# Eight-chunk groups, a ring of 32 slots and one-comparison one-hots in a graph-convolution and expert kernel

## The reference, cut to what matters

```python
def gcn_conv(x, W, b, src, dst, n_nodes):
    loop = jnp.arange(n_nodes)
    s = jnp.concatenate([src, loop])
    d = jnp.concatenate([dst, loop])
    deg = jax.ops.segment_sum(jnp.ones(s.shape[0]), d, num_segments=n_nodes)
    dinv = jnp.where(deg > 0, jax.lax.rsqrt(deg), 0.0)
    xw = x @ W
    msg = xw[s] * (dinv[s] * dinv[d])[:, None]
    return jax.ops.segment_sum(msg, d, num_segments=n_nodes) + b
```

## Time and profile before

| | |
|---|---|
| median of 3 runs | 6199.94 us (6199.23 to 6201.64) |
| profiled execution, its span | 6262.0 us, 79540 instructions |
| layer 1 gathers, 217.5 to 2681.3 us | 2463.8 us |
| between the layers, 2681.3 to 2761.7 us | 80.4 us |
| layer 2 gathers, 2761.7 to 5227.5 us | 2465.8 us |
| before, and behind them | 217.5 us, 1034.5 us |

### The profile page before, as it was taken

The page is one execution under the profiler, slowest core; times in us unless marked ns, Lnnn a source line. Parts: engine busy times, 40 slices in busy tenths (PEclk is TensorE's granted clock), DMA queues, the critical chain, the costliest instruction groups (busy, mean ns, idle before and its releaser), DMA issues.

```text
span 6262.0 us, 79540 instructions
## 1 busy us (share of the span) xinstructions
PE 4364.0 (70%) x15129; PEld 2132.3 (34%) x15130; DVE 1873.3 (30%) x7104; ACT 1178.2 (19%) x2841; POOL 3402.7 (54%) x3639
## 2 busy tenths in 40 slices
PE   4667766676676666666666766667667666669999
PEld 4322222222222222232222222222222223458888
DVE  7311121111121111241122221212121215657776
ACT  5200000000000000030000000001000003545555
POOL 0466666666666666636666666666666663331111
PEclk5676676666666777676776666766666667779999
DMA  3633333333333333343333333333333233331111
GB/s 112 208 106 90 88 88 88 88 89 88 88 90 89 89 87 88 89 126 90 87 90 88 88 89 89 87 89 89 89 87 90 86 90 86 88 116 49 51 48 46
DMA packets 261631, 564.59 MB, mean 90 GB/s; under 512 B 67215, under 2 KB 136177, under 8 KB 261554
## 3 DMA queue, kind: packets, MB, share of 16 engines
q0 software_dynamic: 171168, 466.40, 25.7%
q1 hardware_dynamic: 89234, 95.13, 5.4%
q10 hardware_dynamic: 1152, 2.20, 0.1%
HBM read 503.38 MB, written 60.10 MB: 90 GB/s over the span
## 4 chain that ended last, share of the span: by engine, by line
PE 25%; issue 15%; another core or an unknown queue 14%; DMA 5%; DVEq 4%; POOL 3%; DVE 3%; ACT 2%; ACTq 0%; POOLq 0%; SPq 0%
PE ps L1708 10%; PE ps L1914 7%; DMA ring<-messages,idx_stage 5%; PE ps L1929 3%; POOL ring L645 3%; PE ps L1606 2%; DVEq L1169 2%; DVE onehot_mem L1161 2%; PE ps L1729 1%; PE ps L1833 1%; DVEq L1161 1%; ACT acc L825 0%; ACT dinvT L857 0%; DVEq L1170 0%
## 5 line engine op out<-in xcount | busy, mean ns | idle before, releaser
L645 POOL DMA_INDIRECT ring<-messages,idx_stage x3328 | 3159.0, 949 | 1935.8 <-issue 883.7
L1708 PE MATMUL ps<-ring,onehot_mem 128*64 128x256 f32 x6656 | 2801.3, 544 | 1255.3 <-DMA ring<-messages,idx_stage 621.4
L1708 PEld LDWEIGHTS ps<-ring,onehot_mem 128*64 128x64 f32 x6656 | 950.1, 180 | 2751.8 <-DMA ring<-messages,idx_stage 1650.1
L1172 DVE TENSOR_TENSOR acc<-acc,ps 128x128 f32 x832 | 240.3, 289 | 3795.7 <-remote 2064.5
L779 ACT ACTIVATE win_rows<-ps 64x256 f32<-64x256 f32 x832 | 313.7, 378 | 2224.7 <-PE ps L1708 1106.2
L1161 DVE TENSOR_SCALAR onehot_mem<-iota_bf,tables 128x64 f32<-128x64 bf16 x3344 | 641.8, 268 | 187.5 <-issue 125.7
L1606 PE MATMUL ps<-ident,win_rows 64*128 64x64 f32 x1664 | 337.9, 296 | 368.3 <-ACT win_rows L779 295.7
L768 ACT ACTIVATE idx_stage<-tables 128x8 int32 (+1 forms) x420 | 87.4, 209 | 2276.7 <-PE ps L1708 981.1
L1606 PEld LDWEIGHTS ps<-ident,win_rows 64*128 64x128 f32 x1664 | 206.3, 173 | 867.8 <-issue 867.8
L1914 PE MATMUL ps<-acc 128*128 128x256 f32 x2016 | 459.0, 380 | 0.8 <-ACT acc L955 0.8
L704 POOL DMA_INDIRECT out_dram<-acc x126 | 125.7, 998 | 579.1 <-DVE acc L1556 399.1
(11 more groups left out here) (264 smaller groups left out, 2072.9 us busy)
## 6 DMA issues: line engine op xcount, KB each, us to landing
ring<-messages,idx_stage POOLq DMA_INDIRECT x3328
rows_mem<-in_x_dram SPq DMA_DIRECT2D x54, 448.0 KB, 3.8
acc<-routed_rows SPq DMA_DIRECT2D x63, 268.0 KB
messages<-dinvT SPq DMA_DIRECT2D x23, 448.0 KB, 6.2
dinvT<-in_x_dram SPq DMA_DIRECT2D x22, 448.0 KB, 4.4
messages<-ring SPq DMA_DIRECT2D x19, 448.0 KB, 4.0
dinvT<-dinv_row SPq DMA_DIRECT2D x28, 224.0 KB
messages<-rows_mem SPq DMA_DIRECT2D x14, 448.0 KB, 4.0
```

The source lines that it names most:

```text
L645: pool.indirect_dma_start(out=slots[:, s, :], out_offset=None, in_=t_dram[layer], in_offset=bass.IndirectOffsetOnAxis(ap=idx_stage[:, u, s ...
L1172: dve.tensor_tensor(sums(w, WIN), sums(w, WIN), ps[:, 2 + u, 0:KH * WIN].rearrange("p (k w) -> p k w", k=KH), ALU.add).then_inc(ev_fast, 1)
L1708: pe.matmul(ps[0:WIN, u, 0:D], onehot[:, u, j, 0:WIN], slots[:, s, :], start=j == 0, stop=j == CPG - 1).then_inc(chunks_used, 1)
```

## The change

- `CPG` goes from 4 to 8 and `WIN` from 64 to 128: a group is 8 chunks and its window 128 nodes. There are 208 groups in a layer, and still 1664 chunks, 26 strides of 64 chunks and 28 node chunks.
- The ring has 32 slots (4 groups). They do not fit in `ring`, so the slots and the one-hots lie in the memory of `dinvT`, which is now called `spare`. `dinv` is then no longer resident in a layer: SP loads one node chunk of it a stride into `dinv_now`, the last two into `dinv_last`, and the whole row, in three pieces, between the layers.
- POOL waits for `groups_used`, once in 8 gathers, and the gather of group g needs group g-4 done. PE increments `groups_used` once a group and waits for landings four at a time (`got`, one semaphore for four slots).
- ACT stages row numbers 16 columns at a time in 4 buffers, three blocks ahead.
- The one-hots of a group are one DVE instruction: a `tensor_tensor` comparison of the ramp, repeated over the 8 chunks, with the 8 columns of `relT`, repeated over the window; 1024 elements a partition.
- The hardware loops of four groups inside a stride are written out. DVE waits for the stores of `messages_1` before the one-hots of layer 1, since these now overwrite memory that the stores read.

```diff
-CPG = 4
+CPG = 8
-WIN = 64
+WIN = 128
-SLOTS = 8
+RING = 4
+SLOTS = RING * CPG
+STAGE = 16
+QUAD = 4
+STAGE_BUFS = 4
...
-        slots = ring[:, 0:SLOTS * D].rearrange("p (s f) -> p s f", s=SLOTS)
+        slots = spare[:, 0:SLOTS * D].rearrange("p (s f) -> p s f", s=SLOTS)
+        onehot_mem = spare[:, SLOTS * D:SLOTS * D + CPG * GWIN]
+        dinv_now, dinv_last = spare[:, dinv_at:dinv_at + CH], [spare[:, dinv_at + n * CH:dinv_at + (n + 1) * CH] for n in (1, 2)]
...
+            def dinv_load(run):
+                def load(out, t, done):
+                    sp.dma_start(out, dinv_row[:, bass.ds(t * CH, CH)].to_broadcast([P, CH])).then_inc(done, 16)
+                for n in range(2):
+                    load(dinv_last[n], STRIDES + n, dinv_last_in)
+                load(dinv_now, 0, dinv_in)
+                with sp.Fori(1, STRIDES) as t:
+                    sp.wait_ge(lin_scaled[run], t)
+                    load(dinv_now, t, dinv_in)
...
+            sp.wait_ge(agg_done, 1)
+            for n, (t0, t1) in enumerate(DINV_PARTS):
+                if t1 == NCH:
+                    sp.wait_ge(lin_scaled[L1], NCH)
+                sp.dma_start(dinv_all[:, t0 * CH:t1 * CH], dinv_row[:, t0 * CH:t1 * CH].to_broadcast([P, (t1 - t0) * CH])).then_inc(dinv_part[n], 16)
...
+                    for s in range(STAGE):
+                        c = n * STAGE + s
+                        if c % CPG == 0:
+                            g = i * (STAGE_BUFS * STAGE // CPG) + c // CPG
+                            wait(pool, groups_used, g - RING + 1 + layer * NG)
+                            hold(pool)
                         pool.indirect_dma_start(
-                            out=slots[:, s, :], out_offset=None, in_=t_dram[layer],
-                            in_offset=bass.IndirectOffsetOnAxis(ap=idx_stage[:, u, s:s + 1], axis=0),
-                        ).then_inc(got[s], 16)
+                            out=slots[:, c % SLOTS, :], out_offset=None, in_=t_dram[layer],
+                            in_offset=bass.IndirectOffsetOnAxis(ap=idx_stage[:, n, s:s + 1], axis=0),
+                        ).then_inc(got[c % SLOTS // QUAD], 16)
...
                 def make_onehot(g, u):
-                    for j in range(CPG):
-                        last = dve.tensor_scalar(onehot[:, u, j, 0:WIN], iota_bf[:, 0:WIN],
-                                                 relT[:, bass.ds(g * CPG + j, 1)], None, ALU.is_equal)
-                    last.then_inc(oh_fast, 1)
+                    shape = [P, CPG, WIN]
+                    dve.tensor_tensor(onehot[:, u, :, :], iota_bf[:, 0:WIN].unsqueeze(1).to_broadcast(shape),
+                                      relT[:, bass.ds(g * CPG, CPG)].unsqueeze(2).to_broadcast(shape),
+                                      ALU.is_equal).then_inc(oh_fast, 1)
...
+            dve.wait_ge(dinv_part[0], 16)
             scale_y(0)
...
                 def landed(s, use):
-                    pe.wait_ge(got[s], 16 * (use + done // SLOTS + 1))
+                    if s % QUAD == 0:
+                        pe.wait_ge(got[s // QUAD], 16 * QUAD * (use + run * (NG // RING) + 1))
...
                     for j in range(CPG):
-                        s = (q * CPG + j) % SLOTS
-                        landed(s, i * 2 + (q * CPG + j) // SLOTS)
-                        pe.matmul(ps[0:WIN, u, 0:D], onehot[:, u, j, 0:WIN], slots[:, s, :],
-                                  start=j == 0, stop=j == CPG - 1).then_inc(chunks_used, 1)
+                        landed(q * CPG + j, i)
+                        last = pe.matmul(ps[0:WIN, u, 0:D], onehot[:, u, j, 0:WIN], slots[:, q * CPG + j, :],
+                                         start=j == 0, stop=j == CPG - 1)
+                    last.then_inc(groups_used, 1)
```

204 lines of the change are left out of this document (110 added, 94 removed).

## The result

The changed kernel took 6112.58 us (median of 4 runs, 6106.28 to 6125.07) against 6199.58 us before: a ratio of 0.9861 with a 95% interval from 0.9849 to 0.9873, 1.4% faster. The forecast was 5725 us with a range of 5450 to 6000. The direction was right, and the size was not: 87 us were gained where 475 were forecast, and the time lies outside the range. A second thing came out that the forecast had no place for: on four chips of the later runs the kernel before takes 5440 to 5451 us instead of 6200, and on the one of them where the changed kernel was run as it is, it is 3% slower.

A forecast was written before the change was run, and what follows sets the result against it. POOL's 1.25 us a gather and waits for ring slots were taken as the bound. 6262.0 - 769.6 + 252 + 8 + 4 = 5756 us profiled, or 5694 without the surplus; the middle, 5725 us, was forecast, range 5450 to 6000.

The forecast's parts named there:

- What bounds the kernel: In both gather stretches, POOL's 1.25 us a gather (2080 us a stretch) takes turns with waits for slots, 770 us.
- I take all 770 us as gone: In the gather stretches, the ring of 32 slots removes all of POOL's waits for slots, 769.6 us less.
- The ring's cover: With 32 slots, PE may be some 24 us late before POOL waits; the longest earlier wait was 14.3 us.
- rival B: Gather stretches: late releases grow with the group; a third of the old waiting stays, 5982 us; chance 0.18.
- The comparison: Beside the gathers, DVE's two-SBUF-input one-hot comparison holds up POOL's gathers, 0.605 us a group, 252 us (0 to 512).
- its cheapest way to be wrong: Phase: PE's pace locks the one-hot comparison to one point of POOL's step, making its price anywhere from 0 to 512 us.
- Rival A: Gather stretches: the one-hot comparison does not hold up the gathers, 5473 us; chance 0.2.
- `dinv` and the ends: Between the layers, loading the whole `dinv` row adds 8 us; later finishing of each layer's last group adds 4 us.
- The profiled surplus: Whole kernel: the profiled execution was 62.1 us longer than the runs; half was put into the waits that go away.
- C: Gather stretches: delays above 14.2 us in every second group make the kernel slower, 6570 us; chance 0.04.
- D: Gather stretches: the deeper ring isn't used because something else holds POOL; time stays at 6200 us; chance 0.03.
- Slower than before: Whole kernel: the outcome of being slower by more than about 0.2%; chance 0.04.

The follow-up runs named there:

- e1 to e4: First follow-ups to the changed kernel: eight one-hot comparisons, 5448.8 us; 16 of 32 slots, 5593.6 us; a memset POOL waits for before each gather, 7794.8 or 8230.4 us.
- v1 to v3: Changed kernel with the ramp in PSUM: alone 5450.1 us; plus a 128 x 2 memset ahead of each gather 5472.8 us; with 16 of 32 slots 5450.4 us.

## Why the prediction was right or wrong

**What bounds the kernel.** Right: 1.25 us a gather is POOL's floor. The stretches of the kernel before are 2081 us where nothing is late, against 2080 by the count from the earlier trace rows. Also right that the 770 us are waits for slots, since they are what the other chips do not have: 1935.8 - 1180.6 = 755 us of idle time.

**"I take all 770 us as gone".** This is the step that failed. In the changed kernel 1627.1 us of idle time stand against some 1181 without late updates (the run with eight comparisons on chip 15, the one with PSUM on chip 3). So 446 us of waiting are left, 59% of the 755, and it is 309 us that went. The ring's cover was counted about rightly (24, measured 25.5 us). Wrong was to take the delays of the earlier trace rows (7.0 us on average, 14.3 at most) as events whose length the change would leave alone, so that a longer cover would swallow them. In the changed kernel they last 18.6 us on average and up to 39.2. That is rival B, "the late releases grow with the group". It was given 0.18 and a third of the waiting, and its argument against itself, that the old delays fit under the new cover, was the same mistake. That the delays grew is shown. What sets their length is not: that they last until POOL has to stop fits 71 of the 111 long ones and the spells on chip 5, but 40 ended while POOL went on, and a run with nothing but the ring changed is missing where updates are late.

In the sum for a profiled execution this step outweighs all others: the measured 6123.3 us are 367 above 5756. 769.6 - 308.7 = 461 us of waits stayed; the comparison cost 252 - 166 = 86 us less than was added for it, and the load of `dinv` 8 less.

**The comparison.** The mechanism was right and its size too large: 252 us in the sum, 165.7 in the trace, 149 between two kernels on chip 2. The formula, 1.23 x 1.23 / (2 x 1.25), lets every meeting cost up to 1.23 us. The traces show that a start in the first 0.16 us of a gather costs nothing, and a later one costs its distance less 0.16. By that a start at random costs (1.25 - 0.16) x (1.25 - 0.16) / (2 x 1.25) = 0.475 us, an estimate of 198 us in 416 groups. In the trace of the first measurement the starts are indeed spread over the whole step: of the 350 comparisons that begin where POOL issues without a stop, a quarter begins before 0.22 us and a quarter after 1.15. The meeting at random was not far off there, so most of the miss of this term is the first 0.16 us. On chip 2, where half of the starts lie between 0.45 and 0.80 us, POOL's step and the comparison are tied, which the prediction named as its cheapest way to be wrong. Rival A (no hold-up at all) is refuted by the 1217 ns comparison beside 945 ns gathers once one input is in PSUM.

**`dinv` and the ends.** 8 us were taken for the load between the layers, at 208 GB/s. DVE does not wait for it: the largest piece, 4032 KB, landed in 15.3 us, which is some 270 GB/s. From the end of the last gather of layer 1 to the first of layer 2 it is 84.9 - 0.95 = 84.0 us instead of 80.4. The surplus stands ahead of DVE's first addition behind the last gather, a window that was seen late again, 3.5 us after POOL had stopped:

```profile
2609.45 0.42 DVE L1205 TENSOR_TENSOR acc<-acc,ps 128x256 f32 x1 [21.93 <-issue]
```

On chip 2 the stretch between the gathers is 81.1 us with the changed kernel and 82.2 with the one before. So the term is 0. The 4 us for the ends cannot be seen apart from the 4.3 us that are left over.

**The profiled surplus.** Half of the 62.1 us were put into the waits that go. After the change the profiled execution is 10.7 us above the median. But the two are not alike: after, the profiled execution is itself one of the four runs, before it is a separate one. So these numbers don't tell where the surplus lay.

**Rivals C and D.** C (6570 us) did not come, although its condition, delays over 14.2 us, did. Its price was for delays in every second group. Here one of 18.6 us comes once in 2390.5 / 78 = 31 us, that is in every third group, and most of it is covered. D (the ring isn't used) is excluded: POOL goes on for 26.6 us after PE has turned to other work, which is the ring's doing. **Slower than before** was given 0.04 for one mechanism, and on chip 2 it is the outcome, by another: where nothing is late, the gain isn't there and the comparison's price is. The version with 16 slots, which has the same comparison, is 2.8% slower on chip 15 too. The trace held the hint. It showed that DVE and ACT saw PE late without a reason in the program. A wait with no reason in the program can be one that the same program doesn't have on another chip.

**Still open.** What on chip 5 makes PE slow and its updates late. The runs link it to POOL's gathers (in both kernels it often ends some 3 to 6 us after they stop, though not always) and show that it is no property of the program alone. How it depends on POOL's pace, and how 16 slots compare with 32 with nothing else changed, was not measured there, since the sets that would tell it (e1 to e4, v1 to v3) fell to other chips. Whether the ramp in PSUM brings its 150 us on that chip too is open for the same reason.

## What to carry to other kernels

A delay read in a trace may be as long as it is because of the very thing that is to be changed: before a deeper ring is credited with swallowing a delay, ask what ends the delay, and look whether it ends when POOL stops. A long VectorE instruction that runs beside GpSimd's indirect DMAs should have at most one input in SBUF. Here putting the other into PSUM made it free, and cutting it into short instructions made it cheap. And a gain that rests on a wait with no named releaser should be measured on a second chip before it is believed.

## What the runs showed of the hardware that was not expected

- The kernel before takes 5440 to 5451 us on chips 15, 2, 8 and 3 and 6206 us on chip 5 (9 runs, 6199 to 6210), with the same program. On chip 5 DVE's unnamed waits are there in every kernel that was run. This is the changed kernel with 20 added products:

```profile
L1205 DVE TENSOR_TENSOR acc<-acc,ps 128x256 f32 x416 | 175.1, 421 | 4115.2 <-remote 2782.1 <-PE ps L1653 1010.1 <-issue 322.9
```

- The stage behind the gathers is hit too. It has POOL's scatters in it and is the same code in both measurements of the changed kernel: 6123.3 - 5080.3 = 1043.0 us in the first, 5599.0 - 4622.1 = 976.9 us on chip 2.
- A wait of POOL for its own memset costs 0.79 us ahead of a gather. The same memset costs next to nothing (0.007 us) where POOL waits only for the memsets of a group ago.
- Against the kernel before, eight two-input comparisons of 128 elements cost 0.07 us a group (29.5 / 416) and one of 1024 elements 0.39 (161 / 416); against eight one-input ones it is 0.36 (149 / 416).
- On chip 2 a gather that has begun is not held up by a two-input comparison that begins behind its start, not even one that begins 0.05 us behind it. Only the next one is, and only if the comparison begins more than 0.16 us behind the first one's start.
